# VectorE transposes that write whole 32x32 blocks in place, read with a stride by the next operation

## The reference

```python
def _L0_attn_ref(hidden_states, ...):      # 4096 rows, H = 32 heads of D = 32
    q = (hidden_states @ wq.T + bq).reshape(B, S, H, D)
    k = (hidden_states @ wk.T + bk).reshape(B, S, H, D)
    v = (hidden_states @ wv.T + bv).reshape(B, S, H, D)
    scores = jnp.einsum('bshd,bstd->bsht', q, k) / np.sqrt(D).astype(np.float32)
    probs = jax.nn.softmax(scores, axis=-1)
    context = jnp.einsum('bsht,bstd->bshd', probs, v).reshape(B, S, E)
    return context
...
    x = L0_attn_hidden_states              # (2, 2048, 1024)
    x = x + _L0_attn_ref(_layernorm(x, axis=-1), ...)
    x = x + _L0_ffn_ref(_layernorm(x, axis=-1), ...)   # base product + top-2 of 8 experts, rank 16
    return x
```

## Time and profile before

| | us |
|---|---|
| three timed runs | 1360.42, 1361.67, 1361.64 |
| their median | 1361.64 |
| the profiled execution | 1360.58 |
| its span, first to last instruction | 1358.4 |
| PE busy | 1297.6 (96%) |
| DVE busy | 1077.9 (79%) |
| ACT busy | 689.0 (51%) |
| POOL busy | 259.8 (19%) |
| mean granted clock of PE | 0.987 |

### The profile page before, as it was taken

How to read it: one execution, slowest core, us unless ns; L and a number is a source line. 1 busy time by engine, 2 the same in 40 slices (tenths; PEclk the granted TensorE clock), 3 DMA queues, 4 the chain that set the end, 5 groups by cost and what they waited for, 6 DMA issues and landing times.

```text
span 1358.4 us, 29896 instructions
## 1 busy us (share of the span) xinstructions
PE 1297.6 (96%) x12446; PEld 688.9 (51%) x12446; DVE 1077.9 (79%) x1556; ACT 689.0 (51%) x987; POOL 259.8 (19%) x239
## 2 busy tenths in 40 slices
PE   4767999999999999999999999999999999999996
PEld 1443555555555555555555555555555555555553
DVE  5878887887788778877887887788778877887874
ACT  6774445544454555445445544454555445445531
POOL 0011121222112122221121222112122221121220
PEclk9988999999999999999999999999999999999998
DMA  9521111111111111111111112111111111111110
GB/s 368 206 78 38 64 57 46 46 62 62 62 49 45 60 46 46 62 62 62 41 52 46 46 62 62 62 50 45 59 47 47 62 62 62 40 52 46 31 48 31
DMA packets 33047, 87.41 MB, mean 64 GB/s; under 512 B 6656, under 2 KB 7680, under 8 KB 33024
## 3 DMA queue, kind: packets, MB, share of 16 engines
q1 hardware_dynamic: 33024, 87.10, 19.5%
HBM read 53.52 MB, written 16.78 MB: 52 GB/s over the span
## 4 chain that ended last, share of the span: by engine, by line
PE 89%; DVE 4%; ACT 3%; issue 2%; DMA 0%; SPq 0%; POOL 0%; DVEq 0%; ACTq 0%; POOLq 0%
PE acc L1164 23%; PE dense_acc L1274 23%; PE acc L1173 23%; PE attn_ps L1227 7%; PE attn_ps L1235 4%; PE dense_acc L1282 4%; PE low_ps L1257 1%; PE low_ps L1259 1%; PE low_ps L1258 1%; ACT work L342 1%; PE dense_acc L1297 1%; ACT base_parts L540 1%; DVE base_parts L798 1%; DVE v_parts L798 1%; ACT w_hi_q L564 0%
## 5 line engine op out<-in xcount | busy, mean ns | idle before, releaser
L1274 PE MATMUL dense_acc<-base_parts,x 128*128 128x512 f16 x1488 | 334.7, 379 | 0.0
L342 ACT COPY work<-work 32x512 f16<-32x512 f16 x384 | 236.0, 614 | 8.8
L1274 PEld LDWEIGHTS dense_acc<-base_parts,x 128*128 128x128 f16 x1488 | 143.1, 98 | 160.3
L891 DVE SCALAR_TENSOR_TENSOR work<-acc,acc_to_a,biases_sb 128x512 f32<-128x512 f32 x192 | 143.7, 750 | 83.4 <-PE acc L1173 77.8
L677 ACT CAST work<-work 128x1024 f16<-128x1024 f32 x31 | 32.4, 1046 | 338.6 <-DVE work L989 338.6
L487 POOL TENSOR_TENSOR columns<-columns 128x1 f32<-128x1 f32 x33 | 18.1, 549 | 647.1 <-DVE columns L841 647.1
L1164 PE MATMUL acc<-w_hi_q,x_hi 128*128 128x512 f16 x496 | 118.9, 383 | 5.9 <-DVE work L891 5.9
L1164 PE MATMUL acc<-w_hi_k,x_hi 128*128 128x512 f16 x496 | 120.5, 387 | 2.4 <-issue 2.4
L1173 PE MATMUL acc<-w_hi_q,x_lo 128*128 128x512 f16 x496 | 118.4, 382 | 0.0
L1173 PE MATMUL acc<-w_hi_k,x_lo 128*128 128x512 f16 x496 | 117.2, 379 | 0.0
L1164 PE MATMUL acc<-v_parts,x_hi 128*128 128x512 f16 x496 | 117.2, 379 | 0.0
(11 more groups left out here) (184 smaller groups left out, 2065.1 us busy)
## 6 DMA issues: line engine op xcount, KB each, us to landing
work<-x_dram SPq DMA_DIRECT2D x64, 512.0 KB, 3.5
work<-work SPq DMA_DIRECT2D x256, 64.0 KB, 2.0
out_dram<-work SPq DMA_DIRECT2D x31, 512.0 KB, 2.9
work<-wT_dram SPq DMA_DIRECT2D x17, 512.0 KB, 5.6
v_parts<-wT_dram SPq DMA_DIRECT2D x8, 512.0 KB, 13.8
base_parts<-wT_dram SPq DMA_DIRECT2D x5, 512.0 KB, 10.8
biases_sb<-bias_dram SPq DMA_DIRECT2D x4, 512.0 KB, 7.5
base_parts<-agT_dram SPq DMA_DIRECT2D x1, 544.0 KB, 9.7
```

The lines of the kernel that those rows point to most:

```text
L342: copy(diag[c * QD:(c + 1) * QD, :, c, j::NQ, :], src).then_inc(vdiag_ready, 1)
L891: nc.vector.scalar_tensor_tensor(out=ev[:, s], in0=acc[bank][:, :], scalar=acc_to_a[:, i:i + 1], in1=bias[g][:, s], op0=ALU.mult, op1=ALU. ...
L1274: nc.tensor.matmul(dense_acc[n][:, :], rows_part[:, k, :], w_part[:, k, cols], start=(k == 0 and m == 0), stop=False)
```

## The change

A new view `turned_back` reads `turned` with 32 elements between neighbours: value (b, a) lies at a*32+b. The k and q transposes now read `ev` in order and write `turned` in order. The v and context transposes still read with the stride and write in order. All that read `turned` after k, q, v and the context read `turned_back`, so with a stride of 128 bytes between neighbouring 32-bit values: three ACT copies, two POOL subtractions and two DVE operations in a step. The softmax transpose and its readers stay. No instruction is added, removed or put elsewhere, on any engine; neither are waits. The list of instructions is the same, with other access patterns on those named.

```diff
+        turned_back = turned.rearrange("p (a b) -> p b a", a=QD)
...
             def second_lo(t):
...
-                nc.gpsimd.tensor_tensor(dense_parts[:, :, 1, :], turned3, dense_parts[:, :, 0, :],
+                nc.gpsimd.tensor_tensor(dense_parts[:, :, 1, :], turned_back, dense_parts[:, :, 0, :],
                                         ALU.subtract).then_inc(b_lo_ready, 1)
...
             def v_low(t):
...
-                nc.gpsimd.tensor_tensor(v_parts_t[:, :, 1, :], turned3, v_parts_t[:, :, 0, :],
+                nc.gpsimd.tensor_tensor(v_parts_t[:, :, 1, :], turned_back, v_parts_t[:, :, 0, :],
                                         ALU.subtract).then_inc(v_lo_ready, 1)
...
-                nc.scalar.copy(k_parts[:, 0, :, :], turned3).then_inc(a_hi_ready, 1)
+                nc.scalar.copy(k_parts[:, 0, :, :], turned_back).then_inc(a_hi_ready, 1)
...
-                nc.scalar.copy(dense_parts[:, :, 0, :], turned3).then_inc(b_hi_ready, 1)
+                nc.scalar.copy(dense_parts[:, :, 0, :], turned_back).then_inc(b_hi_ready, 1)
...
-                nc.scalar.copy(v_parts_t[:, :, 0, :], turned3).then_inc(v_hi_ready, 1)
+                nc.scalar.copy(v_parts_t[:, :, 0, :], turned_back).then_inc(v_hi_ready, 1)
...
             def attention_end(p, x1):
...
-                nc.vector.transpose(turned.rearrange("p (h d) -> p d h", h=HEADS),
+                nc.vector.transpose(turned3,
                                     attn_ps[:, :].rearrange("p (t d) -> p d t", t=QD)).then_inc(ctx_turned, 1)
...
-                nc.vector.scalar_tensor_tensor(out=x1, in0=turned, scalar=ctx_undo[:, 0:1], in1=res, op0=ALU.mult,
-                                               op1=ALU.add).then_inc(x1_ready, 1)
+                nc.vector.scalar_tensor_tensor(out=x1.rearrange("p (h d) -> p h d", h=HEADS), in0=turned_back,
+                                               scalar=ctx_undo[:, 0:1], in1=res.rearrange("p (h d) -> p h d", h=HEADS),
+                                               op0=ALU.mult, op1=ALU.add).then_inc(x1_ready, 1)
...
             def turn_first(t):
...
-                nc.vector.transpose(turned.rearrange("p (t h) -> p h t", t=QD), ev_heads).then_inc(at_ready, 1)
+                nc.vector.transpose(turned, ev).then_inc(at_ready, 1)
...
-                nc.vector.tensor_tensor(k_parts[:, 1, :, :], turned3, k_parts[:, 0, :, :],
+                nc.vector.tensor_tensor(k_parts[:, 1, :, :], turned_back, k_parts[:, 0, :, :],
                                         ALU.subtract).then_inc(a_lo_ready, 1)
...
-                nc.vector.transpose(turned.rearrange("p (t h) -> p h t", t=QD), ev_heads).then_inc(bt_ready, 1)
+                nc.vector.transpose(turned, ev).then_inc(bt_ready, 1)
...
-                nc.vector.transpose(turned.rearrange("p (t d) -> p d t", t=QD),
+                nc.vector.transpose(turned3,
                                     ev.rearrange("p (h d) -> p d h", h=HEADS)).then_inc(vt_ready, 1)
```

More of the change, by code:

```diff
@@ L1013, in first_step @@
                 dve.wait_ge(a_lo_ready, 1)
-                nc.vector.transpose(turned.rearrange("p (t h) -> p h t", t=QD), ev_heads).then_inc(bt_ready, 1)
+                nc.vector.transpose(turned, ev).then_inc(bt_ready, 1)
                 split("v", w_hi["v"], w_lo["v"])
                 dve.wait_ge(b_hi_ready, 1)
-                nc.vector.tensor_tensor(dense_parts[:, :, 1, :], turned3, dense_parts[:, :, 0, :],
+                nc.vector.tensor_tensor(dense_parts[:, :, 1, :], turned_back, dense_parts[:, :, 0, :],
                                         ALU.subtract).then_inc(b_lo_ready, 1)
```

## The result

The changed kernel takes **1403.64 us** (median of 4 runs, 1403.29 to 1405.07) where the kernel before took 1361.22 on the same chips (4 runs): a ratio of 1.0315, 95% interval 1.0299 to 1.0332, 42.4 us more. The forecast was 1398.6, with a range of 1374 to 1422. The profiled execution took 1403.55, its span is 1401.4, 43.0 more than before.

What follows compares the result with a forecast made beforehand. PE was taken to bound the loop; 29 steps, each with 1.22 us of waiting at the scores, give 35.4, with 1.6 outside +37.0, so 1397.6 for the profiled execution and 1398.6 us as median; range 1374 to 1422.

Steps and rivals of the forecast that it cites:

- The bound and the chain: Loop: PE always busy; turn2, centre, q copy, low part of q, scores form a fixed-length chain the change lengthens.
- The slack: At the loop's scores: POOL's low part of q could end 0.16 us later before PE waits.
- The transposes: DVE: k and q 0.73 us shorter each, context 0.70, v 0.2 (to 1.98); hidden beside PE in the loop.
- ACT's read: ACT's q, k and v copies: 0.74 us longer each, bounds 0 and 0.95; the q copy costs 0.64 a step.
- POOL's read: POOL's low parts of q and v: 0.74 us longer, bounds 0 and 1.24; q's costs 0.58 a step.
- The v path: v transpose to ACT's spreads before the context: 0.69 us of cover, costed at 0, up to 0.6 a step otherwise.
- Outside the loop: Step 0, step 1, step 31 and tail: -0.7, +1.5 and +0.8, together +1.6 us.
- The rival on the clock: PE's clock falls with the loop's new gaps: at least 1.7 us more a step, 1450 us or more; chance 0.03.
- Free reads: Strided reads cost nothing on any engine, the transposes' gains stay: 4.0 us faster, 1357.6 us; chance 0.11.
- Only one engine pays: In the q chain only ACT or only POOL is slower: 1375 us for ACT, 1378 for POOL; chance 0.16.
- Upper bounds: ACT's q copy grows by 0.95 and POOL's low part by 1.24 us: 1422 us; chance 0.13.
- +50%: POOL's reads over 8 bytes apart: low part of q grows by 1.06 us, whole forecast by some 9 us.

Runs made afterwards that it cites:

- e1: Changed kernel with q put back (its transposes write with the stride, its readers read in order), k, v and context still changed: 1364.43 us, ratio 1.0025.
- e2: Kernel before with q alone changed: transposes in order, ACT's copy and POOL's low part read with the stride; 1400.44 us, ratio 1.0290.
- e6: Changed kernel with ACT's q copy moved ahead of centre's last operation and POOL's low part of q ahead of row_root, steps 1 to 31: 1380.33 us.
- e3: Kernel before with only ACT's q copy reading with the stride, in steps 1 to 31: 1381.13 us, ratio 1.0146.
- e4: Kernel before with only POOL's low part of q reading its 32-bit input with the stride: 1375.09 us, ratio 1.0101.
- e7: No layer computed: strided reads on ACT, DVE and POOL, DVE transposes, and DVE beside POOL timed alone; ACT's copy 1044 ns at distance 1, 1985 at 4.

## Why the prediction was right, point by point

- **The bound and the chain.** PE bound with one chain near it, of `turn2`, `centre`, q copy, low part of q and scores: shown by e1, e2 and e6. **The slack** of 0.16 us at the scores is shown by e3 and e4, whose costs add up to 0.16 less than the whole.
- **The transposes.** k 0.74, context 0.70 gained, as said; v 2.05 against 1.98. None of this made the loop shorter, as said.
- **ACT's read**: 0.74 was taken, it is 0.92, near the upper end of 0.95. The price of a strided write on DVE was the wrong measure: a strided read costs ACT more than DVE, since ACT is faster in order (1029 ns against 1226) and both end near 1.9 us for 1024 columns. The prediction had called ACT's stream the slower one, which the earlier trace rows did not bear out. **POOL's read**: 0.74 was taken, it is 0.61. Both misses together: 1.25 instead of 1.22 a step, 29 x 0.03 = 0.9 us. They nearly cancelled, which was luck: alone, 0.18 and 0.13 a step would have been 5.2 and 3.8 us.
- **The v path.** Its cover was costed at 0 of up to 0.6; it held (18.07 and 18.08 us from scores to context, the last spreads at 14.99 both times), and e1, whose loop has no wait, shows it.
- **Outside the loop**: 1.6 was forecast, and it is 43.0 - 29 x 1.25 = 6.8. This term was mis-sized. Up to the scores of step 1 it was 0.8, measured 1.3; in step 1 nothing beside the loop's 1.25, measured 2.8; for step 31 0.1, measured 0.2; behind its scores 0.7, measured 2.5. So of the 5.2 missing, 2.8 are PE's lower clock in step 1, and 1.8 lie in the tail. The rival on the clock was put at 0.03 for the whole loop; at gaps of 1.2 us it did not happen, but nobody asked for the gaps that were long already. In step 1 the sum said that PE's wait of 1.89 would grow by 1.5, and did not follow what 3.4 or more do. The tail is alike: +0.9 until the context can start, behind ACT's spreads (14.68 to 15.60 us from the scores), where 0.7 was forecast; then 96 matmuls in 2.08 instead of 1.52 us, and more slow ones. In step 0, the 0.7 us from the q transpose did not arrive either: the scores there start 0.46 earlier (79.32 and 78.86), but after a wait of 3.35 us instead of 0.59, and take 2.75 instead of 1.52. That wait is not the change's alone: e6, whose step 0 is the changed kernel's, has 0.61, and e3 and e4, whose step 0 is the old one, have 2.08 and 1.88. What sets it was not tested.
- **The rivals.** Free reads: refuted on SBUF, true on PSUM. Only one engine pays: refuted by the groups, and what each alone costs was put at 1375 and 1378 and measured, by e3 and e4, at 1381 for ACT and 1375 for POOL. Upper bounds: right for ACT (0.95 and 0.92), twice too high for POOL (1.24 and 0.61). The rule of the Trainium skill's GPSIMD Engine Reference (section 7), +50%, was too high as well; here it is +28%. The clock: at gaps of 1.2 us it stayed up through the loop; the 1450 of that rival is its 29 x 1.7 = 49 on top of 1398.6, rounded up from 1448.

## What to carry to other kernels

A stride moved from one operation to its readers is not gone: count who reads, and how near each reader is to the engine that bounds. Look for the chain that starts from the bounding engine and ends at it, and measure its slack with one operation's end, one start and one handover; 0.16 us here decided over 3%, while four faster transposes were worth nothing in the loop. Where a longer operation must enter such a chain, its place in its engine's order can give back most of what it costs: 0.83 of 1.25 us in e6.

## What the runs showed of the hardware that was not expected

- **Distance 2 is free, distance 4 is not**, for reads on three engines (table above). Writes were timed at distance 32 alone.
- **Small operations of DVE stand still beside POOL.** In the changed kernel a conversion of 8 numbers takes 1622 ns on average, where it took 236. The timelines of DVE, first before, then after, where POOL's v part runs from 670.01 to 672.74:

```profile
650.65 0.25 DVE L930 CAST best_no<-best_at 128x8 f32<-128x8 uint32 x1
```

```profile
670.85 0.16 DVE L929 FIND_INDEX8 best_at<-best,logits 128x8 uint32<-128x8 f32 x1
671.04 1.73 DVE L931 CAST best_no<-best_at 128x8 f32<-128x8 uint32 x1
```

  Before, it began 0.22 us ahead of POOL's end (650.87), now 1.70 us; both times it ends with POOL, within 0.03 us, while the search just before it is not held up. The Trainium skill's GPSIMD Engine Reference (section 8, key points) says that POOL and DVE share their ways to SBUF and get in each other's way when DVE's instruction uses two ports or has two SBUF inputs. The addition of e7 has two inputs in SBUF, and stands, as that section says; whether conversion, copy and scaling use two ports, no run here shows. It cost nothing here: e2 has the short conversion (236 ns) and the step of the whole change, e1 the long one (1629 ns) and the step of the kernel before.
- **PE's clock after a wait** does not follow from the length of that wait: 2.90 us left it up, 2.78 us did not. What else counts stays open.
